# A gated cross-attention and feed-forward block on one core: all steps of the main loop in a new order

## The reference, cut to what matters

```python
def xattn(q, k, v, ...):                      # k and v are both the context
    f_q, f_k, f_v = (proj(q), proj(k), proj(v))   # layer norm, then @ w_in.T: 8 heads of 128
    cosine_sim = dots(f_q, f_k) / (|f_q| * |f_k|)
    var_component = q_ratio * k_ratio         # from the variance of every row of f_q and f_k
    # decorr_scale and the three weights cw, vw, ww are sums over the whole input, one per head
    mixed = cw * cosine_sim + vw * cosine_sim * decorr_scale + ww * var_component
    return (mixed @ f_v) @ w_out.T + b_out    # no softmax

def ffn(x, Wq, Wk, Wv, Wo, Wff):              # 16 heads of 16
    q, k, v = x @ Wq, x @ Wk, x @ Wv
    attn = softmax(over queries, k q.T / 16)
    z = l2_normalize(l2_normalize((attn.T @ v) @ Wo) @ Wff)
    return gelu(z)                            # exact gelu

x = x + tanh(g_xattn) * xattn(layernorm(x), context, context)
x = x + tanh(g_ffn) * ffn(layernorm(x))
```

## Time and profile before

| | us |
|---|---|
| median of 3 runs (1378.04 to 1384.31) | 1383.85 |
| the profiled execution's own time | 1381.58 |
| its span, first to last instruction | 1379.9 |
| PE busy | 1200.6 (87%) |
| DVE busy | 1110.5 (80%) |
| ACT busy | 1013.5 (73%) |
| POOL busy | 196.5 (14%) |

### The profile page before, as it was taken

How to read it: one execution, slowest core, us unless ns; L and a number is a source line. 1 busy time by engine, 2 the same in 40 slices (tenths; PEclk the granted TensorE clock), 3 DMA queues, 4 the chain that set the end, 5 groups by cost and what they waited for, 6 DMA issues and landing times.

```text
span 1379.9 us, 34693 instructions
## 1 busy us (share of the span) xinstructions
PE 1200.6 (87%) x10386; PEld 753.0 (55%) x10386; DVE 1110.5 (80%) x3180; ACT 1013.5 (73%) x3334; POOL 196.5 (14%) x160
## 2 busy tenths in 40 slices
...
GB/s 253 145 143 19 10 45 76 155 91 142 116 137 121 121 137 92 166 69 189 53 205 30 210 32 210 34 210 48 195 63 178 80 170 88 154 104 153 92 154 16
DMA packets 247888, 162.30 MB, mean 118 GB/s; under 512 B 94538, under 2 KB 235559, under 8 KB 247848
## 3 DMA queue, kind: packets, MB, share of 16 engines
...
## 4 chain that ended last, share of the span: by engine, by line
PE 39%; DVE 14%; issue 10%; SPq 9%; DMA 9%; ACT 2%; DVEq 1%; POOLq 0%; POOL 0%; ACTq 0%
PE work L893 11%; PE work L895 10%; PE work L894 10%; DMA sqE<-sq_rows 5%; PE attended L1455 4%; SPq L1280 4%; DVE nm L1733 4%; DMA sq_rows<-sqT 3%; PE score L1444 2%; SPq L1288 2%; DVE md L1687 2%; PE work L1351 2%; DVE mTl L1640 1%; DVE norm L1629 1%; SPq L1309 1%
## 5 line engine op out<-in xcount | busy, mean ns | idle before, releaser
L1540 ACT ACTIVATE prob<-score,nm 128x256 f32<-128x256 f32 x1024 | 474.1, 481 | 48.5 <-DVE nm L1733 39.5
L1733 DVE TENSOR_REDUCE nm<-score 128x2 f32<-128x512 f32 x512 | 337.7, 679 | 38.4 <-PE score L1444 38.2
L1540 ACT ACTIVATION_READ_ACCUMULATOR prob<-score,nm 128x1 f32 x1024 | 218.0, 213 | 0.0
L1455 PE MATMUL attended<-prob,vsp 128*32 128x256 f32 x2048 | 135.2, 393 | 14.3 <-DVE vsp L1748 8.4
L1444 PE MATMUL score<-qstack,kstack 64*128 64x256 f16 x1024 | 98.2, 280 | 38.0 <-ACT prob L1540 35.6
L1653 DVE BATCH_NORM_STATS2 qst<-work 128x6 f32<-128x128 f32 x512 | 111.5, 281 | 7.5 <-PE work L895 7.3
L893 PE MATMUL work<-xTh,Gh 128*128 128x256 f16 (+1 forms) x320 | 89.7, 280 | 20.4 <-DVE md L1687 19.7
L1687 DVE SCALAR_TENSOR_TENSOR md<-work,rkc,sqE 128x256 f32<-128x256 f32 (+1 forms) x160 | 70.9, 477 | 44.6 <-DMA sqE<-sq_rows 36.0
L893 PE MATMUL work<-wTh,xTh 128*128 128x512 f16 x256 | 97.9, 383 | 5.0 <-DVE xTl L1647 3.5
L894 PE MATMUL work<-wTl,xTh 128*128 128x512 f16 x256 | 97.8, 382 | 0.0
L895 PE MATMUL work<-wTh,xTl 128*128 128x512 f16 x256 | 97.6, 381 | 0.0
...
## 6 DMA issues: line engine op xcount, KB each, us to landing
...
```

The costliest lines, as they stand in the source:

```text
L1455: last = nc.tensor.matmul(pvb[32 * j:32 * j + 32, t, :], vsp[:, k, (4 * e + j) * 2 * FD:(4 * e + j + 1) * 2 * FD], prob[:, n % PG, e, j, : ...
L1540: nc.scalar.activation(prob[:, g % PG, e, j + jj, :], sc[n % SC][:, jj * NQ:(jj + 1) * NQ], ACT.Exp, bias=nm[:, u + jj:u + jj + 1], accum_ ...
L1733: nc.vector.tensor_reduce(nm[:, u:u + 2], sc[n % SC][:, :].rearrange("p (u q) -> p u q", q=NQ), AX.X, ALU.max, negate=True).then_inc(max_r ...
```

## The change

`ORDER`, `HEAD` and `TAIL` are replaced. Both orders hold the same 264 steps. `MOVED` changes with them: `V1`, `X0`, `M1`, `back2` and `pv1` now work on another pair than before, `rk`, `G1.h` and `G1.l` and `G2.l` belong to other turns. Two small things go with it: the count that a `.l` step waits for is taken from `ORDER` also in the head and the tail, and each of the six projections `pq`, `pk`, `pv` now waits for `zz0` and `zz1` to be drained, where only the first of them did. What each instruction computes is unchanged.

```diff
@@ -948,45 +948,45 @@
 
 
 ORDER = """
-pv1.v res qs2 V2 G3 V2.h a0 X0 V2.l back1 G0 G3.h M1 G3.l a0.v X1 M2 V1 V4 G0.h aux V1.h M3 G0.l V1.l sqe0 X2 S2 M4 M5
-V0 a1 V4.h V4.l X3 V0.h X4 a1.h R0 S3 V5 P0 X5 M6 V0.l V5.h V3 V3.h a1.l M7 sqe1 X6 V5.l S4 M8 d0 M9 d1 V3.l X7 vt0 X8
-d0.o ldy R1 d2 X9 S5 wq d1.o m0.h vt1 M10 M11 m1.h m0.l m1.l X10 P1 X11 S6 E0 fk1 M12 fk1.h M13 X12 d2.o fk1.l d3 d3.o
-S7 d4 M14 m2.h m2.l d5 M15 ldx X13 X14 fk0 S8 L0 R2 P2 m3.h d4.o M16 m3.l M17 X15 m4.h S9 y0 d5.o X16 z M18 X17 fk0.h
-R3 S10 m5.h M19 zT0 fk0.l P3 X18 y0.o m4.l m5.l M20 zT0.h fk2 X19 zT1 zT0.f fk2.h zT0.l E1 fk2.l S11 R4 M21 zT1.h
-back3 y1 zT1.f zT1.l q0 M22 X20 X21 rk M23 y1.o q1 q0.o q2 L1 X22 O0 ln1 X23 S12 R5 q1.o M24 O0. q2.o lpow P4 M25 ln2
-P5 q3 q3.o q4 X24 zz0 S13 X25 q4.o M26 S14 zz0.h zz1 q5 zz1.h zz0.l q6 X26 M27 zz1.l X27 M28 E2 X28 M29 X29 q5.o S15
-M30 q6.o M31 R6 X30 pq0 X31 L2 pq0.h pk0 q7 R7 pk0.h pq0.l pk0.l P6 P7 O1 E3 L3 q7.o O1. O2 O3 qs1 O2. parts0 pk1
-back0 O3. G4 pq1 pk1.h pk1.l F1 G4.h G4.l qpow pq1.h G5 F2 G5.h back2 pq1.l G2 G2.h G5.l G2.l F3 G1 pv0 parts1 S0
-pv0.v M0 F4 S1 pv1 G1.h out G1.l
+G0 X1 G1.h M2 G2.l G0.h qs2 G3 G3.h ldx S2 M3 G1.l G0.l G3.l a0 X2 a0.v res V3 V5 pv1 V3.h M4 V5.h aux back1 M5 V3.l
+V0 X3 rk X4 V5.l z back2 pv1.v R0 S3 V4 V0.h fk0 V4.h X5 P0 M6 S4 X6 M7 V0.l V4.l fk0.h X7 sqe0 V2 M8 sqe1 fk0.l M9
+V2.h fk1 V2.l R1 X8 X9 S5 fk1.h vt1 a1 d0 M10 M11 X10 fk1.l vt0 S6 M12 a1.h P1 a1.l fk2 X11 d0.o E0 S7 fk2.h m0.h M13
+d1 L0 d2 R2 P2 X12 fk2.l M14 m0.l M15 X13 X14 d3 X15 d1.o d2.o S8 m1.h M16 d4 R3 m2.h M17 S9 m1.l X16 m2.l d3.o wq ldy
+d5 X17 d4.o P3 E1 S10 zT0 M18 m3.h zT0.h m4.h M19 y0 X18 m3.l m4.l X19 d5.o m5.h M20 zT1 zT0.f zT1.h L1 m5.l M21 zT0.l
+S11 y0.o M22 y1 X20 zT1.f M23 R4 zT1.l y1.o X21 X22 ln1 O0 X23 R5 back3 O1 q0 S12 S13 P4 O0. P5 lpow q0.o M24 M25 M26
+O1. M27 q1 q2 ln2 q1.o q3 X24 q2.o q3.o zz0 X25 X26 X27 S14 S15 M28 zz1 zz0.h zz0.l E2 zz1.h q4 X28 M29 q5 zz1.l q4.o
+M30 pk0 X29 X30 q6 q5.o M31 X31 pq0 pk0.h L2 R6 pq0.h R7 pk0.l P6 q6.o P7 q7 pq0.l E3 L3 O2 q7.o O2. O3 G5 qs1 pq1 O3.
+G5.h G5.l F1 F2 parts0 pq1.h V1 V1.h back0 pk1 S0 pq1.l G4 V1.l F3 M0 pk1.h pk1.l G4.h G4.l G1 M1 parts1 X0 F4 pv0
+pv0.v qpow G2 S1 G2.h out
 """.split()
 
 HEAD = """
-fk1 rk fk0 fk1.h fk1.l fk0.h fk0.l ldx fk2 z fk2.h zT0 zT1 fk2.l zT0.h zT0.f zT1.h zT0.l zT1.f zT1.l q0 q0.o q1 q2
-q1.o q3 q2.o q3.o q4 G5 q4.o q5 q5.o +ldx q6 q6.o G4 G4.h G4.l q7 G2 G5.h G5.l G2.h q7.o qs1 G1 G1.h qpow G2.l G1.l
-+V2 +G3 +qs2 +V2.h +a0 +V2.l +a0.v +G0 +G3.h +G3.l +G0.h +V4 +V1 +V1.h +G0.l +V4.h +ldy +V1.l +V4.l +V0 +V0.h +a1 +V5
-+a1.h +V5.h +V0.l +aux +V3 +sqe0 +a1.l +d0 +V3.h +V3.l +V5.l +d1 +d0.o +sqe1 +fk1 +d2 +d1.o +m0.h +m0.l +d2.o +fk1.h
...
+ldx fk0 fk1 fk0.h fk1.h +ldy fk1.l z fk2 fk2.h fk2.l zT0 zT0.h zT1 zT0.f zT0.l zT1.h fk0.l zT1.f zT1.l q0 q1 q2 q0.o
+q1.o q2.o q3 q3.o q4 q5 q4.o q6 q5.o q6.o q7 q7.o G5 G4 V1 G5.h V1.h G4.h qs1 qpow G4.l G2 V1.l G5.l G1 G2.h +G0 +G2.l
++G1.h +G3 +G0.h +G0.l +G3.h +G1.l +qs2 +G3.l +V3 +a0 +V5 +a0.v +V3.h +V3.l +V5.h +V5.l +V0 +V0.h +fk0 +fk0.h +V4 +V0.l
++fk0.l +rk +a1 +ldx +V4.h +V4.l +V2 +V2.h +V2.l +fk1 +aux +z +d0 +fk1.h +sqe0 +d0.o +sqe1 +a1.h +vt0 +a1.l +d1 +fk1.l
++m0.h +m0.l +fk2 +fk2.h +d1.o +m1.h +fk2.l +d2 +m1.l +d3 +d2.o +d3.o +d4 +m2.h +m2.l +d5 +d4.o +m3.h +m3.l +m4.h +d5.o
...
 TAIL = """
-V2 back1 back3 qs2 pv1.v M1 X0 V2.h G3 G3.h X1 a0 V2.l res a0.v M2 G0 aux S2 G0.h G3.l V1 M3 X2 sqe0 X3 M4 M5 V1.h
-G0.l V4 V4.h V0 S3 R0 V1.l a1 X4 V0.h M6 V4.l a1.h P0 V5 X5 S4 V5.h sqe1 M7 X6 X7 a1.l d0 V0.l M8 V5.l S5 M9 X8 ldy R1
...
+qs2 G2.l G0 G1.h back2 X1 G0.h G3 G3.h G1.l M2 M3 a0 a0.v S2 G0.l V3 G3.l V5 pv1 M4 X2 X3 V3.h V3.l aux M5 V5.h X4 V0
+V5.l S3 pv1.v V4 V0.h back1 R0 rk M6 V0.l res X5 S4 M7 V4.h X6 X7 P0 V4.l V2 sqe0 a1 V2.h M8 M9 X8 V2.l R1 S5 d0 sqe1
...
 """.split()
 
-MOVED = {step: n for n, steps in {0: "G1 G1.h G1.l G2 G2.h G2.l G4 G4.h G4.l G5 G5.h G5.l qpow qs1 rk", 1: "M0 S0 S1", 2: "back1 back3 pv1.v res"}.items() for step in steps.split()}
+MOVED = {step: n for n, steps in {0: "G1 G2 G2.h G4 G4.h G4.l G5 G5.h G5.l V1 V1.h V1.l qpow qs1", 1: "M0 M1 S0 S1 X0", 2: "back1 back2 back3 pv1 pv1.v res"}.items() for step in steps.split()}
 CHUNKS = [s for s in ORDER if any(t.startswith(s + ".") for t in ORDER)]
 A_INDEX = {name: k for k, name in enumerate(CHUNKS)}
 WORK_USES = [len(range(s, len(CHUNKS), WORK)) for s in range(WORK)]
@@ -1013,11 +1013,6 @@
 def halves(order, n):
 
     return [s[:-2] for s in dict.fromkeys(map(plain, order)) if s.endswith(".h") and s[:2] != "zT" and lead(s) == n]
-
-
-def first_projection(order):
-
-    return next(s for s in map(plain, order) if s in ("pq0", "pk0", "pv0"))
 
 
 def last_use(n, slots, count):
@@ -1149,7 +1144,7 @@
     def halved(e, pair):
 
         n = lead(e + ".h")
-        done = halves(running["order"], n)
+        done = halves(ORDER, n)
         return hi_ready[n], pair * len(done) + done.index(e) + 1
 
     def emptied(e, half):
@@ -1178,15 +1173,12 @@
 
         return qk[kind[1]][half][:, c, :], bk[:, :], (1.0 / 16 if kind == "pq" else 1.0) / WS
 
-    running = {"order": ORDER}
-
     def run(eng, a_part, b_part, passed=None):
 
         def part_of(s, pair):
             (b_part if late(s) else a_part)(s, pair)
 
         def short_turns(first, order):
-            running["order"] = order
             waiting = [[(first + n, s) for n in range(2) for s in CHUNKS[slot::WORK]] for slot in range(WORK)]
 
             def pass_over(slot, upto=None):
@@ -1210,7 +1202,6 @@
                 pass_over(slot)
 
         short_turns(0, HEAD)
-        running["order"] = ORDER
         with eng.Fori(0, NPAIR - 2) as i:
             for s in ORDER:
                 part_of(s, i + 2 - lead(s))
@@ -1405,14 +1396,12 @@
                                             mT, (slice(0, Y_ROWS[t]), c, t, slice(r * P, (r + 1) * P)),
                                             Vp, (slice(0, Y_ROWS[t]), c, t), t == 0, t == HT - 1)
                 elif kind in ("pq", "pk"):
-                    if e == first_projection(running["order"]):
-                        wait_drained(pe, a, "zz0", "zz1")
+                    wait_drained(pe, a, "zz0", "zz1")
                     for k in range(KT):
                         last = products(nc, bk[:, :], w["w" + kind[1]], (ALL, k, slice(c * P, (c + 1) * P)), zzT, (ALL, k),
                                         k == 0, k == KT - 1)
                 elif kind == "pv":
-                    if e == first_projection(running["order"]):
-                        wait_drained(pe, a, "zz0", "zz1")
+                    wait_drained(pe, a, "zz0", "zz1")
                     for r in range(2):
                         for k in range(KT):
                             last = products(nc, bk[:, r * DIM:(r + 1) * DIM],
```

More of the change, by code:

```diff
@@ L970 @@
-+ln1 +q2 +q0.o +q1.o +q2.o +q3 +lpow +ln2 +q3.o +q4 +zz0 +zz0.h +q4.o +zz1 +zz0.l +zz1.h +q5 +zz1.l +q5.o +pq0 +pq0.h
-+pk0 +q6 +pq0.l +pk0.h +pk1 +pk0.l +pk1.h +q6.o +q7 +pk1.l +parts0 +G4 +G4.h +G5 +q7.o +G5.h +qs1 +pq1 +back0 +pq1.h
-+G4.l +G2 +G5.l +pv0 +G2.h +pq1.l +G1 +G2.l +pv1 +G1.h +qpow +S0 +S1 +parts1 +G1.l +M0 +pv0.v +back2
+ldx fk0 fk1 fk0.h fk1.h +ldy fk1.l z fk2 fk2.h fk2.l zT0 zT0.h zT1 zT0.f zT0.l zT1.h fk0.l zT1.f zT1.l q0 q1 q2 q0.o
+q1.o q2.o q3 q3.o q4 q5 q4.o q6 q5.o q6.o q7 q7.o G5 G4 V1 G5.h V1.h G4.h qs1 qpow G4.l G2 V1.l G5.l G1 G2.h +G0 +G2.l
@@ new lines @@
++G1.h +G3 +G0.h +G0.l +G3.h +G1.l +qs2 +G3.l +V3 +a0 +V5 +a0.v +V3.h +V3.l +V5.h +V5.l +V0 +V0.h +fk0 +fk0.h +V4 +V0.l
++fk0.l +rk +a1 +ldx +V4.h +V4.l +V2 +V2.h +V2.l +fk1 +aux +z +d0 +fk1.h +sqe0 +d0.o +sqe1 +a1.h +vt0 +a1.l +d1 +fk1.l
++m0.h +m0.l +fk2 +fk2.h +d1.o +m1.h +fk2.l +d2 +m1.l +d3 +d2.o +d3.o +d4 +m2.h +m2.l +d5 +d4.o +m3.h +m3.l +m4.h +d5.o
++vt1 +zT0 +wq +zT0.h +zT1 +zT0.f +zT1.h +m4.l +zT0.l +zT1.f +m5.h +y0 +m5.l +y1 +y0.o +zT1.l +y1.o +ln1 +q0 +q1 +q0.o
++q1.o +lpow +q2 +ln2 +q3 +zz0 +zz0.h +q2.o +q3.o +zz0.l +zz1 +q4 +zz1.h +zz1.l +q5 +q4.o +pk0 +q5.o +pq0 +pk0.h +pq0.h
@@ L973 @@
++q6 +pk0.l +pq0.l +q6.o +q7 +q7.o +pq1 +pq1.h +parts0 +G5 +back0 +pq1.l +G5.h +G4 +V1 +V1.h +G5.l +qs1 +qpow +G4.h
++pk1 +G4.l +G2 +pk1.h +S0 +V1.l +G2.h +pk1.l +pv0 +M0 +X0 +parts1 +S1 +M1 +G1 +pv0.v
 """.split()
 TAIL = """
-V2 back1 back3 qs2 pv1.v M1 X0 V2.h G3 G3.h X1 a0 V2.l res a0.v M2 G0 aux S2 G0.h G3.l V1 M3 X2 sqe0 X3 M4 M5 V1.h
-G0.l V4 V4.h V0 S3 R0 V1.l a1 X4 V0.h M6 V4.l a1.h P0 V5 X5 S4 V5.h sqe1 M7 X6 X7 a1.l d0 V0.l M8 V5.l S5 M9 X8 ldy R1
-X9 P1 M10 S6 M11 X10 d0.o X11 V3 M12 V3.h M13 E0 X12 R2 X13 d1 V3.l S7 M14 L0 P2 M15 S8 m0.h X14 vt0 d1.o m1.h m0.l
@@ L978 @@
-M16 d2 d3 d2.o X15 M17 S9 m1.l d4 m2.h M18 X16 wq M19 d5 X17 m2.l X18 S10 vt1 R3 X19 d3.o d4.o M20 m3.h m4.h m3.l M21
-P3 m4.l E1 X20 X21 S11 d5.o M22 m5.h y0 S12 m5.l M23 M24 X22 y0.o y1 M25 X23 R4 L1 R5 S13 y1.o P4 P5 O0 X24 E2 ln1
-lpow M26 X25 O0. M27 X26 ln2 S14 M28 zz0 X27 M29 zz0.h zz1 zz1.h zz0.l X28 S15 zz1.l L2 pq0 M30 M31 X29 X30 X31 pk0 R6
```

(2 more changed lines are left out.)

16 lines of the change are left out of this document (10 added, 6 removed).

## The result

The changed kernel took 1332.97 us (median of 4 runs, 1331.18 to 1335.55) beside 1384.08 us for the kernel before (4 runs, 1378.04 to 1385.94). The ratio is 0.9639 with a 95% interval of [0.9604, 0.9674]: 51 us faster. The forecast was 1374 us with a range of 1350 to 1399.

What follows compares the result with a forecast made beforehand. No engine is full (PE 87% busy); step order around the turn's boundary decides. New waits 3.75 + 1.4 + 0.7 = 5.85 us replace 6.43; 1381.6 - 8 - 2 = 1371.6, named 1374 for the median; range 1350 to 1399.

Steps and rivals of the forecast that it cites:

- What goes: PE's marked idle time around the turn's boundary, waits for `v`, `sqE` dots, exponentials and banks: all 6.43 us open to be replaced.
- Term 1: End of the turn on PE: `pv0` waits for `pk1.l` behind `F3` on ACT; PE idles about 3.75 us.
- Term 2: ACT then late after `pk1.h`, so PE waits at `G0`, `G3`, `a0`, `V3`: 1.4 us.
- Term 3: `ldx` and `back2` join SP's crowded loads, so `back1` lands late for `S4`: 0.7 us, ends 0 and 3.3.
- the forecast's 0.58: Net gain per turn in us: new waits of 5.85 in place of 6.43; 8 us in 14 turns.
- Head and tail: Ahead of the loop 2 us off, from more cover before `a0`; behind it 0, within 4 us either way.
- The five extra waits for `zz0` and `zz1`: Five more steps with two waits each, on semaphores reached long before: taken as 0, up to 1 us a turn.
- The gap at `pv0` closes: Rival: `pk1` finishes and `G4`, `G1` start later, or ACT passes `F3` earlier; 2 us not 3.75, 1349; chance 0.20.
- Nothing moves: Rival: the loop's waits only change places, the three engines' loads being the same; 1384 us; chance 0.11.
- The third table load: Rival: each loop body gets a load at its start, `X1` 1.28 us later; 18 us, 1392; chance 0.14.

## Why the forecast was too small

**What goes (6.43 us).** Right, and by the chains named: 0.41 us of PE waiting for `v` in place of 1.71, none at the dots, 11 us for exponentials over the span in place of 35.6, no `d.o` wait for `sqE`. What the forecast did not see is how they hang together. `aux` had two releasers that ended within 0.1 us of each other in the trace of before, and it named one of them, SP's, for the `sqE` wait, and the other, ACT's, for `v` alone. The experiments give the `sqE` wait 32 of the 51 us. The other 19 are not split by a run. By the turns (69.63 and 68.68 us on average) 13 of them are the loop's. The waits that the old order without `sqE`'s kept (1.72 + 0.51 + 0.78 + 1.03 + 0.95 = 5.0 us a turn) against 3.74 in the new order's usual turn make 1.3 us, less 0.6 us that PE is busy longer in the new one (64.94 for 64.3); that is a count from traces, and it falls 0.3 us a turn short.

**Term 1 (3.75 us at `pv0`) is the step that failed.** The wait is there and for the reason named, split around `S0` and `G4`, but it measured 1.48 + 0.44 = 1.92 us, 1.83 less, 26 us in 14 turns. The chain from `O3.` to `pk1.l` was put at 7.7 us with `F1`, `F2`, the load, the Gelus and the halves in series. In the trace it is 6.1 (455.34 to 461.41), because the load (457.21 to 458.49) runs while `F2` does, and `F2` takes 1.2 us and not 1.6. The rest is PE's work in the stretch, 4.2 us for 3.95. I read "`F2` until the load starts at 473.87" as a dependence. The trace of before had the rows against it: `F2` is done at 473.65, and the load comes right behind the halves on ACT, at 473.86.

```profile
473.49 0.16 DVE L1763 TENSOR_TENSOR fac<-fac 128x4 f32<-128x4 f32 x1
473.10 0.76 ACT L1513 ACTIVATE Gh<-work 128x308 f16<-128x308 f32 x2
```

The run with the load forced into series brought 1.35 of the 1.83 us back. Of the 1.92 us, 1.48 stand at `S0`, which I had counted as work for PE without asking when `back0` lands (3.4 us from the issue at 455.88). By the constant sum above this cost nothing: without it `pv0` would have waited for all of it.

**Term 2 (1.4 us at `G0`, `G3`, `a0`, `V3`)** measured 0.28 + 0.41 = 0.69 us, 0.71 less, 10 us in 14 turns. It was built on the late ACT of term 1.

**Term 3 (0.7 us for the DMA crowd)** is nothing in the turn read and 0.50 + 0.27 = 0.77 us in the next, the usual one, where DVE's `z` waits 1.13 us for `xin` (0.54 in the turn read) and `P0` and a `V` stand behind it. The size was right, the place (`S4`) wrong. The forecast's 320 GB/s at full share, worked out from 0.85 and 273, did not come: at a share of 1.06 the stretch moved 275 GB/s, so the DMA engines had no 15% left for the added loads.

**Not foreseen.** `y0` has 0.36 us of issue time, and PE is busy 0.33 us more in the turn (64.94 for 64.61). Together with the forecast's 0.58 and the terms, 0.58 + 1.83 + 0.71 + 0.70 - 0.36 - 0.33 = 3.13 us, and 71.39 - 68.25 is 3.14. With term 3 in place, as in most turns, it is 0.6 us less (68.86). The forecast had nothing for the clock, some 3 us over the loop.

**Head and tail.** 2 us were forecast ahead of the loop, 3.9 came; 0 (4 either way) behind it, 2.2 came. The head of before has some 3 us at half clock too (227 to 231, behind a wait of 2.13 us for `md`), the one after none from 206 us on. What each part gave is not split by a run. The five extra waits for `zz0` and `zz1` show nowhere in PE's rows: 0, as taken.

**The rivals.** "The gap at `pv0` closes" (1349) was the nearest: it had term 1 at 2 us, 1.92 came, and its condition, that ACT gets through `F3` earlier, is what happened; term 2 fell with it, so it was itself too small. ("Nothing moves" counted 63 us of work for DVE; the earlier trace rows has 61.4.) The third table load did not come:

```profile
L1553 ACT ACT_TABLE_LOAD x16 | 20.5, 1283 | 0.3
L1529 ACT ACT_TABLE_LOAD x15 | 19.2, 1283 | 0.3
```

Two a turn, at `F3` and at `X0`, none at `X1`. On the drain of 1380 ns that the Trainium skill adds to a switch (page "ScalarE: Activation LUTs", section "What ACT_TABLE_LOAD costs"): the trace after has the Gelus 0.02 us behind the load's end again, so neither trace shows the drain, and the new order without any switch is no faster, 1331.38 against 1332.49.
